# Macaron block on one core: the second product of the expert layers four quarters behind the first, with twenty more quarters split by VectorE

## The reference

```python
def ffn(x):                                   # x: [2048, 128], 8 experts, hidden 512
    probs = softmax(x @ router_w.T)           # top 2 of 8, renormalised to top_w, top_idx
    h = relu(einsum('tc,efc->tef', x, w1) + b1)      # first product, all 8 experts
    y = einsum('tef,ecf->tec', h, w2) + b2           # second product
    return sum over the 2 chosen experts of top_w * y

def attention(x):
    # mixes of x and the token before it, projections r, w, k, v, g, then per head and token:
    #   kv = k_t[:, None] * v_t[None, :];  o_t = q_t @ (S + u * kv);  S = exp(w_t) * S + kv
    # group norm of o, times silu(g), times W_o

x = x + 0.5 * ffn(layernorm(x))
x = x + attention(layernorm(x))
x = x + 0.5 * ffn(layernorm(x))
```

## Time and profile before

| | |
|---|---|
| median of 3 runs | 491.13 us (491.0 to 491.53) |
| the profiled execution's own time | 491.48 us |
| its span in the trace | 489.6 us |
| PE busy | 477.3 us (97%) |
| DVE busy | 367.5 us (75%) |
| ACT busy | 338.0 us (69%) |
| POOL busy | 240.8 us (49%) |
| HBM traffic | 90 GB/s over the span |

### The profile page before, as it was taken

How to read it: one execution, slowest core, us unless ns; L and a number is a source line. 1 busy time by engine, 2 the same in 40 slices (tenths; PEclk the granted TensorE clock), 3 DMA queues, 4 the chain that set the end, 5 groups by cost and what they waited for, 6 DMA issues and landing times.

```text
span 489.6 us, 6291 instructions
## 1 busy us (share of the span) xinstructions
PE 477.3 (97%) x1873; PEld 302.0 (62%) x1873; DVE 367.5 (75%) x714; ACT 338.0 (69%) x569; POOL 240.8 (49%) x252
## 2 busy tenths in 40 slices
PE   8999999999999999999999999999999999999996
PEld 4676776566557556555755755565566565777775
DVE  3889877759975895997496799935669994667644
ACT  3776787677757668773857767646778765687874
POOL 3235632627875162886516268834616874321322
PEclk9999999999999999999999999999999999999999
DMA  7771121058410017730003555111046611003200
GB/s 252 233 269 33 54 64 41 7 154 234 129 43 1 1 44 208 204 106 1 1 2 129 150 175 151 44 64 43 1 120 182 195 43 44 0 1 117 79 1 21
DMA packets 21297, 44.59 MB, mean 91 GB/s; under 512 B 3856, under 2 KB 4240, under 8 KB 21264
## 3 DMA queue, kind: packets, MB, share of 16 engines
q1 hardware_dynamic: 14928, 32.66, 21.5%
q10 hardware_dynamic: 6336, 11.54, 8.3%
HBM read 40.91 MB, written 3.28 MB: 90 GB/s over the span
## 4 chain that ended last, share of the span: by engine, by line
PE 58%; issue 16%; POOL 11%; DVE 10%; ACT 3%; DMA 1%; POOLq 0%; ACTq 0%; DVEq 0%
PE Y L377 12%; PE U L346 8%; PE U L350 7%; PE U L347 7%; POOL qs L955 5%; PE Y L368 4%; PE Y L373 4%; PE Y L370 4%; POOL xT L929 4%; DVE hid_lo L773 2%; PE A L450 2%; PE A L442 1%; POOL pool_a L961 1%; PE A L436 1%; DVE gy L782 1%
## 5 line engine op out<-in xcount | busy, mean ns | idle before, releaser
L929 POOL TENSOR_TENSOR xT<-xT,gy 128x512 f32<-128x512 f32 x63 | 84.3, 1338 | 146.2 <-DVE gy L782 146.0
L346 PE MATMUL U<-xhi,w1lo 128*128 128x512 f32 x256 | 151.6, 592 | 3.0 <-ACT hid_hi L575 1.2
L377 PE MATMUL Y<-hid,w 128*128 128x512 f32 x264 | 134.2, 589 | 0.0
L773 DVE TENSOR_TENSOR hid_lo<-hid,hid_hi 128x512 fp32r<-128x512 f32 x124 | 97.8, 793 | 39.0 <-ACT hid_hi L575 38.5
L577 ACT ACTIVATE hid<-U,small 128x512 f32<-128x512 f32 x132 | 90.6, 689 | 48.6 <-PE U L350 46.2
L574 ACT ACTIVATE hid<-U,small 128x512 f32<-128x512 f32 x124 | 85.5, 690 | 43.8 <-PE U L350 39.3
L350 PE MATMUL U<-xlo,w1hi 128*128 128x512 f32 x256 | 100.8, 394 | 0.0
L347 PE MATMUL U<-xhi,w1hi 128*128 128x512 f32 x256 | 100.5, 392 | 0.0
L955 POOL TENSOR_TENSOR qs<-q,pool_a 128x512 f32<-128x512 f32 x64 | 80.1, 1251 | 15.0 <-DVE pool_a L830 14.8
L346 PEld LDWEIGHTS U<-xhi,w1lo 128*128 128x128 f32 x256 | 48.1, 188 | 62.1 <-issue 35.9
L575 ACT ACTIVATE hid_hi<-U,small 128x512 fp32r<-128x512 f32 x124 | 84.8, 684 | 0.0
(11 more groups left out here) (135 smaller groups left out, 515.9 us busy)
## 6 DMA issues: line engine op xcount, KB each, us to landing
G<-gate_dram SPq DMA_DIRECT2D x32, 512.0 KB, 4.3
vb<-v_dram ACTq DMA_DIRECT2D x44, 256.0 KB, 3.6
vb<-v_dram SPq DMA_DIRECT2D x20, 256.0 KB, 4.5
pool_a<-wexp_dram SPq DMA_DIRECT2D x8, 256.0 KB, 6.8
w<-wexp_dram SPq DMA_DIRECT2D x8, 256.0 KB, 6.8
v_dram<-v SPq DMA_DIRECT2D x8, 256.0 KB, 2.2
xnt<-xtok_dram SPq DMA_DIRECT2D x4, 256.0 KB, 5.1
xT<-xT_dram SPq DMA_DIRECT2D x4, 256.0 KB, 7.1
```

The lines of the kernel that those rows point to most:

```text
L346: mm(dst, w1lo[:, e, f, :], xhi[:, k % NB, :], start=True, stop=False)
L377: last = mm(dst, w2[:, g % E, f, :], hid[:, n % HS, cut], start=first, stop=final)
L773: dve.tensor_tensor(hid_lo[:, c, :], hid[:, n % HS, :], hid_hi[:, c, :], ALU.subtract).then_inc(h_lo, 1)
L929: pool.tensor_tensor(xT[:, h, b, :], xT[:, h, b, :], gy[:, g % 2, :], ALU.add).then_inc(acc, 1)
```

## The change

- `LAG` goes from 3 to 4: the second product runs four quarters behind the first. With it `hid` becomes a ring of 6 and each combine stands a slot later. Each unit and nearly all preparations move one slot later too, and the preparation of block 1 four slots (6 to 10).
- `hid_hi` and `hid_lo` become rings of 5. To have room, the gate rows become a ring of 4 experts, so a load of two experts waits for an expert's combine that lies nearer, and two loads, not three, are issued ahead.
- Twenty quarters with n % 4 == 3 (`QUIET`) are split as well. For these ScalarE makes only the plain relu, and VectorE makes the high part by a copy (L798 of the new kernel) ahead of its subtraction. GpSimd splits the fourth quarter of `w2` too, two experts at a time, in slots 33, 37, 39 and 41.
- Three more slots are in `LATE`, the quarters that stay whole (112, 144, 192). With the moved units, 94, 138 and 182 become split and 85 whole. In all 143 quarters are split, 19 more than before.
- Routing is cut into ten steps. Block 1's is spread over ten slots.
- The first load of tokens is cut in two; ScalarE issues the second half.
- At the end VectorE does both halves of the last combine one after the other, GpSimd adds the first half and VectorE the second.

```diff
-PREP = [None, 6, 34, 77, 119, 129, 172, 216]
-UNIT = [37, 79, 121, 165]
+PREP = [None, 10, 35, 78, 120, 130, 173, 217]
+UNIT = [38, 80, 122, 166]
-LAG = 3
+LAG = 4
-HS, QS, SS = 5, 8, 4
-FP, PS, GS, VS = 3, 3, 6, 5
+HS, QS, SS = 6, 8, 4
+FP, PS, GS, VS = 3, 5, 4, 5
+def route_slots(k):
+    return {1: 10, 2: 5, 3: 5}.get(k, 3)
 def route_steps(k, t):
-    if not 0 <= t < route_slots(k):
-        return ()
-    return (t + 1,) if route_slots(k) == 5 else ((1, 2), (3, 4), (5,))[t]
+    return [1 + n for n in range(ROUTE) if n * route_slots(k) // ROUTE == t]
 def combine_slot(g):
-    return 4 * g + {0: 10}.get(g, 7)
-LATE = (slot_of(2, T_PO) + 1, slot_of(2, T_PO) + 5)
+    return 4 * g + {0: 11}.get(g, 8)
+LATE = (112, 144, 164, 168, 192)
+LAST_PARTS = (33, 37, 39, 41)
+QUIET = (47, 51, 79, 83, 87, 91, 119, 123, 127, 131, 167, 171, 175, 215, 219, 235, 239, 243, 247, 251)
+def by_vector(n):
+    return n % FC == FP and n in QUIET
 def in_parts(n):
     scans = any(slot_of(i, T_SC) - 3 <= n < slot_of(i, T_PO if i == UNITS - 1 else T_OUT) for i in range(UNITS))
-    return n >= FC and n % FC < (1 if scans else FP) and n not in LATE
+    return n >= FC and n % FC < (1 if scans else FP) and n not in LATE or by_vector(n)
 # SyncE, head and tail
-            tokens_in(0)
+            sp.dma_start(xnt[:, 0:2, :].rearrange("p t n -> p (t n)"), xtok_in[:, 0:2 * P]).then_inc(tok_in[0], 16)
-                sp.wait_ge(fin, c + 1)
+                if c == 0:
+                    sp.wait_ge(acc, BLOCKS * E)
+                else:
+                    sp.wait_ge(fin, 1)
 # TensorE, ffn_down
+                    if f == FP:
+                        pe.wait_ge(w2lo_s, E + g % E // 2 + 1)
+                        pe.wait_ge(h_lo, parts_to(n + 1))
 # ScalarE
-                if in_parts(n):
+                if in_parts(n) and not by_vector(n):
+            act.dma_start(xnt[:, 2:4, :].rearrange("p t n -> p (t n)"), xtok_in[:, 2 * P:4 * P]).then_inc(tok_in2, 16)
 # VectorE, split_h
                     dve.wait_ge(h_f, n + 1)
+                    if by_vector(n):
+                        dve.wait_ge(down, PARTS[PARTS.index(n) - PS] + 1)
+                        link(dve.tensor_copy(hid_hi[:, c, :], hid[:, n % HS, :]))
                     dve.tensor_tensor(hid_lo[:, c, :], hid[:, n % HS, :], hid_hi[:, c, :], ALU.subtract).then_inc(h_lo, 1)
 # GpSimd
+            def split_w2_last(e):
+                done = E + e // 2 + 1
+                pool.tensor_copy(w2hi[:, e:e + 2, FP], w2[:, e:e + 2, FP]).then_inc(w2hi_s, 1)
+                pool.wait_ge(w2hi_s, done)
+                pool.tensor_tensor(w2lo[:, e:e + 2, FP], w2[:, e:e + 2, FP], w2hi[:, e:e + 2, FP],
+                                   ALU.subtract).then_inc(w2lo_s, 1)
```

More of the change, by code:

```diff
@@ L170, in program @@
         gate_T = sb("gate_T", [P, NB, 32])
-        w2hi = sb("w2hi", [P, E, FP, P], F32R)
-        w2lo = sb("w2lo", [P, E, FP, P], F32R)
+        w2hi = sb("w2hi", [P, E, FC, P], F32R)
+        w2lo = sb("w2lo", [P, E, FC, P], F32R)
         G = sb("G", [P, GS, NT])
@@ L696, in stats @@
                 for t in range(4):
+                    if ln == 0 and t == 2:
+                        dve.wait_ge(tok_in2, 16)
                     src = xnt[:, t0 + t, :] if ln in LOADED else bank[:, t * P:(t + 1) * P]
@@ L760, in route @@
                                                   op0=ALU.mult, op1=ALU.mult))
-                if step == 5:
+                if step == 9:
                     link(dve.scalar_tensor_tensor(out=r(6), in0=r(3), scalar=1e-9, in1=r(4), op0=ALU.add, op1=ALU.add))
                     link(dve.reciprocal(r(7), r(6)))
+                if step == 10:
                     link(dve.tensor_tensor(gate[:, b].rearrange("p e t -> p t e"), m(3), bc(r(7)), ALU.mult))
@@ L793, in finish @@
                     dve.wait_ge(half_y, c + 1)
-                    link(dve.scalar_tensor_tensor(out=gy[:, g % 2, at], in0=bank, scalar=w(W_B2 + g % E, 1),
-                                                  in1=G[:, g % GS, at], op0=ALU.add, op1=ALU.mult))
-                    dve.tensor_tensor(xT[:, h, b, at], xT[:, h, b, at], gy[:, g % 2, at], ALU.add).then_inc(fin, 1)
+                    dve.scalar_tensor_tensor(out=gy[:, g % 2, at], in0=bank, scalar=w(W_B2 + g % E, 1),
+                                             in1=G[:, g % GS, at], op0=ALU.add, op1=ALU.mult).then_inc(comb, 1)
+                dve.wait_ge(comb, g + 2)
+                dve.tensor_tensor(xT[:, h, b, at], xT[:, h, b, at], gy[:, g % 2, at], ALU.add).then_inc(fin, 1)
             def prepare(k, t):
@@ L915, in _ @@
                     attend(i, step_of(i, n))
+            combine(due[ALL])
             split_h(ALL - 1)
@@ L1005, in _ @@
                     split_w2((n // 4 + 1) % E)
+                if n in LAST_PARTS:
+                    split_w2_last(2 * LAST_PARTS.index(n))
                 for i in range(UNITS):
                     attend(i, step_of(i, n))
+            add_y(due[ALL])
+            g = BLOCKS * E - 1
+            h, b = home(BLOCKS - 1)
+            pool.wait_ge(comb, g + 1)
+            pool.wait_ge(acc, g)
+            pool.tensor_tensor(xT[:, h, b, 0:NT // 2], xT[:, h, b, 0:NT // 2], gy[:, g % 2, 0:NT // 2], ALU.add).then_inc(acc, 1)
 def order(m):
```

24 lines of the change are left out of this document (15 added, 9 removed).

## The result

The changed kernel takes 496.91 us (median of 4 runs, 495.1 to 497.84); the kernel before, run beside it, 491.33 (491.0 to 491.6). The ratio is 1.0111, 95% interval [1.0099, 1.0123]: 5.6 us slower, where I forecast 4.5 us faster. The time lies above my range, and the sign is wrong.

A forecast was written before the change was run, and what follows sets the result against it. TensorE was taken to bound the kernel nearly everywhere, if other engines keep up. Terms -3.2 + 1.2 - 1.5 - 0.4 + 0 - 0.4 + 0.2 - 0.3 - 0.1 = -4.5 us gave 486.6 us (485 to 488), overall range 483.2 to 490.2.

The forecast's parts named there:

- `w2` splits: GpSimd's four extra splits in slots 33 to 41 can hold small VectorE norm instructions: +0.2 us (0 to 0.8).
- Fewer passes: On TensorE, 19 more quarters are split, each worth 0.17 us: 3.2 us less.
- The copies at the token mixes: VectorE at the mixes of units 0, 2 and 3: added copies stall 0 to 2.7 us together, taken as +1.2.
- One quarter more of distance: Whole pipeline: all work but first product and relu moves by the same slot, letting copies be late; cost 0.
- Routing of block 1: Early slots: TensorE's pauses up to slot 24 shrink, -1.5 us (0 to -2.3); slot 11's pause goes, -0.4.
- rival B: Only the passes count: early pauses move instead of going, mixes cost 2 us; 489 us, chance 0.17.
- Gate ring: Gate-row loads with a ring of four: cost 0, at most +1 us if a block's first load is late.
- Start of scans: Unit 2's wait for VectorE's scan: 0 (-0.6 to +0.7); unit 1's last reduction, waiting 0.46 us for GpSimd, relieved: -0.4.
- Head: VectorE's first statistics: two token loads of half size may come earlier, -0.3 us (-0.7 to +0.8).
- A: Hand-off fails: copy and subtraction held at mixes of units 0, 2 and 3, 9 us; 494.5 us, chance 0.10.
- The rule: VectorE and GpSimd contend for SBUF ports: all twenty copies and subtractions can be held once, upper bound 61 us on VectorE.
- my low sign: VectorE's copies: an average of 0.45 us would mean the cost at the mixes was taken too dear.

The follow-up runs named there:

- distance with rings: Kernel before with second product four quarters behind, `hid_hi` and `hid_lo` rings of 5, gate rows ring of 4, same 124 split quarters, no copies: 494.45 us.
- without copies: Changed kernel without the twenty quarters split by VectorE and without GpSimd's extra splits of `w2`: 491.9 us.
- the subtractions later: Changed kernel with every VectorE subtraction and copy one slot later, two slots after its relu: 486.75 us.
- the two halves: Two runs on the changed kernel: only the twenty copied quarters one slot later, 493.42 us; only the other 123 subtractions one slot later, 492.59 us.
- distance three: Changed kernel with all subtractions and copies one slot later, but the second product three quarters behind the first again: 512.08 us.
- only the others later: Changed kernel with only the 123 other subtractions one slot later, the twenty copied quarters left one slot behind their relu: 492.59 us.
- the short ring: Kernel before with second product four quarters behind, `hid_hi` left in a ring of 3, gate ring 6, no copies: 507.1 us.

## Why the prediction was wrong

The forecast was -4.5 us and the result is +5.6. The runs divide the 10.1 us between them like this:

| part | forecast | measured | from |
|---|---|---|---|
| distance and rings | 0 | +3.0 | distance with rings, against before |
| twenty quarters with copies, `w2` splits | -3.4 + 1.2 + 0.2 | +4.9 | after, against without copies |
| the rest (routing, other whole and split quarters, head, tail) | -2.5 | -2.3 | without copies, against distance with rings |

The forecast of the passes is 19 x 0.17, or 20 with copies and a net one fewer elsewhere, which the last row has (+0.2).

- **Fewer passes: right.** 1.39 and 1.55 us, 143 split quarters.
- **"The copies at the token mixes", +1.2: the term that failed most.** The measured cost is 8.3, with the splits of `w2` in it (+0.2). Units 0 and 3 lost 0.71 and 0.53 us, inside the ranges that I gave them, by what I had named: copy and subtraction held beside GpSimd ahead of mixes and projection. The rest of the cost lies elsewhere: 2.21 us at the end of unit 0 and the mixes of unit 1, which I had at nothing, and 2.51 in unit 2, for which I had allowed 1. I wrote "in unit 1 the copy of 87 falls where VectorE waits for TensorE's mixes" and priced no other copy near it. Quarter 83's copy stands in front of `o`, and it waits 2.25 us for its relu with the whole queue behind it. I had priced each copy by its length and never asked whether its input is there when the queue comes to it. And I looked at the mixes only, not at the norm behind them, where TensorE's longest wait of slots 121 to 142 stands (0.89 us). Another 1.39 us hang on the late store and may not be the copies' doing.
- **"One quarter more of distance ... I cost it at 0": failed, +3.0.** I wrote that "all work but the first product and its relu moves by the same slot". But the subtraction follows the relu and does not move either. So the combine, two slots ahead of it before, stands one slot ahead now, and more subtractions run beside GpSimd's addition (19 of 61 over 0.9 us, 12 before). This stands in the order of VectorE's instructions, which I compared only at the mixes and at a split of `w1`. The second half of the step, that the distance is what lets VectorE be late, holds: at three the late subtractions cost 25 us more. But the change never used it, since it left the subtractions early.
- **Routing of block 1, -1.5 and -0.4: wrong.** The pauses moved (rival B said so): 0.76, 0.66 and 1.49 us. Undoing the spread changed nothing with the subtractions later. The row "the rest" comes out near my sum by luck, not by my terms: between the two traces 1.4 us of it lie in slots 98 to 121, where a wait of 1.36 us at the end of unit 1's scan is gone and quarter 112 is made whole (I had -0.4), and 0.7 in slots 4 to 44 (I had -1.9). Which edit gives each is not shown by a run of its own.
- **Gate ring at 0: right** on the kernel before; beside the other edits not tested.
- **Start of scans:** TensorE's wait at unit 2 is 0.87 us (0.52 in the earlier trace rows and another 0.54 a slot later, which is gone), the 0.46 us of unit 1's end went as forecast, but those of units 2 and 3 grew by 0.96 us together; with the distance alone they are as long (1.46 and 1.45 us).
- **Head: can't be told.** The first product begins at 9.35 us, before at 9.54, and VectorE's first wait is 3.31 us (3.49 in the earlier trace rows). But with the distance alone, where the load is not cut, it begins at 9.26.
- **The rivals.** A came nearest: slower, with 9 us for the copies. But its mechanism, both instructions held at the mixes of units 0, 2 and 3 with waits of 2 us, is not what the trace shows: units 0 and 3 lost about half a microsecond each, and the longest wait is for a relu. I gave it 0.10 on the ground that "the mixes of unit 1 and all copies elsewhere meet idle VectorE". In the kernel before VectorE idles 38.5 us in front of subtractions, for relus, and I read all of that as slack. Much of it was: VectorE does 38.4 us more work, those waits fall to 14.7 us, and the span grows by 5.4. But such a wait can't be filled by an instruction that waits for the next relu itself, and there the work behind it comes late.
- **The rule.** "Every one of the twenty copies and subtractions can be held once" was the upper bound, and the Trainium skill, "SBUF — State Buffer", "Who interferes with whom", is borne out where they meet: three copies took 1.27 to 1.31 us, the other seventeen 0.41 to 0.43. So holding of the copies themselves adds only 2.6 us of VectorE's time; it does not explain 8.3. The mean copy, 550 ns, lies near my low sign (450), by which I would have said that I took the mixes too dear. That sign misled: the length of the copies did not tell their cost.

Open: how much of the distance's 3.0 us is holding and how much the relu waits; whether the ten microseconds are more than the two halves' 8.0, and by what; what makes the store of `v` late in some traces; what sets the pause before the eighth expert; which of the small edits gives the 2.3 us.

## What to carry to other kernels

On an engine that runs its queue in order, the price of an added instruction is up to its length plus the wait for its input, paid by whoever waits for what stands behind it. Whether a wait is there has to be looked up copy by copy: here one of twenty had a long one. Put the instruction where its input has long been there: one slot more behind the producer, for copies and subtractions alike, was worth 10 us here, with not one instruction less. When a pipeline is made deeper, list what does not move with it (here the subtraction), look at what it stands next to now, and lengthen every ring on the way: one at three against a distance of four cost some 13 us.

## What the runs showed of the hardware

- How often a VectorE instruction meets GpSimd depends on one slot of order: subtractions of the same shape took 0.65 to 1.80 us in the kernel after, and of those n % 4 == 0 12 of 61 were over 0.9 us before, 27 of 58 after and 14 of 58 with all a slot later.
- A float32 product in one piece (two instructions) of 128x512 makes a slot 0.15 to 0.18 us longer than three float32r passes, in the stretches without waits of every kernel here.
- A second relu on ScalarE for twenty quarters (ScalarE 336.2 to 347.8 us busy), with all subtractions later, cost nothing that the runs can tell.
- In three of the kept traces TensorE's granted clock fell from 1.00 to 0.50 for a stretch, each time at a stop of TensorE: of 2.73 and 3.78 us at distance three, of 2.01 with only the others later, of 1.25 and soon 0.43 with the short ring. In the changed kernel no stop, the longest 1.49 us, was followed by one while the slots ran.
- The time from a store of `v` to the loads that wait for it to land differs between traces: at unit 1 it was 3.07 us without copies, 4.35 after and 5.71 with only the others later; with all later it was 4.50, and 3.09 once block 1's routing was put back, which changes no instruction there.
